# A new order of work and new turns in shared buffers, for four chunks of a transformer stack on one core

## The reference, cut to what matters

```python
x = layernorm(x + L0_attn(x))   # a decaying complex scan along the sequence
x = layernorm(x + L0_ffn(x))    # 8 experts, 256 hidden, top 2 by a sparse mixer
x = layernorm(x + L1_attn(x))   # 2 heads of 64, rotary, causal
x = layernorm(x + L1_ffn(x))    # latent attention (4 heads of 32), then 1 shared + 8 experts, 128 hidden
x = layernorm(x + L2_attn(x))   # 16 heads of 8, window of 32
x = layernorm(x + L2_ffn(x))    # dynamics: router, 2 steps of expert-driven control, refinement
x = layernorm(x + L3_attn(x))   # top 16 of 32 keys looked back at, previous key, phrase key
x = layernorm(x + L3_ffn(x))    # 8 experts, 342 hidden, routed by distance to centroids
```

```python
for _ in range(2):
    ctx = concatenate([integrated, v]); ...
    integrated = integrated + halt * (x_next - integrated)
    v = v + halt * (v_next - v)
refined = gelu(integrated @ refine_w1 + b1) @ refine_w2 + b2
out = xf + integration_weight * refined
```

## Time and profile before

| | us |
|---|---|
| median of 3 runs (lowest, highest) | 1227.08 (1224.92, 1227.92) |
| the profiled execution's own time | 1226.56 |
| its span, first to last instruction | 1224.5 |
| PE busy | 1115.4, 91% of the span |
| PE weight loads busy | 629.4, 51% |
| DVE busy | 827.1, 68% |
| ACT busy | 657.6, 54%, of which 186 table loads are 238.6 |
| POOL busy | 219.1, 18% |
| mean granted clock of PE | 0.959 |

### The profile page before, as it was taken

How to read it: one execution, slowest core, us unless ns; L and a number is a source line. 1 busy time by engine, 2 the same in 40 slices (tenths; PEclk the granted TensorE clock), 3 DMA queues, 4 the chain that set the end, 5 groups by cost and what they waited for, 6 DMA issues and landing times.

```text
span 1224.5 us, 16730 instructions
## 1 busy us (share of the span) xinstructions
PE 1115.4 (91%) x5800; PEld 629.4 (51%) x5800; DVE 827.1 (68%) x2446; ACT 657.6 (54%) x1028; POOL 219.1 (18%) x251
## 2 busy tenths in 40 slices
PE   0799967799999999999799989999999999999996
PEld 0455544566554455554455555454464553565554
DVE  6987566489577369868486696678584774664534
ACT  0225344555756766677666575668546655542321
POOL 1312042224021214131200150005020000202000
PEclk9899989899989989997899999799999999999999
DMA  7021100121110000001001111001001010111210
GB/s 268 4 73 54 39 14 14 30 68 34 33 48 24 27 14 21 20 27 33 1 14 56 37 37 37 1 18 37 18 28 37 18 37 1 45 36 54 79 56 9
DMA packets 45394, 45.91 MB, mean 37 GB/s; under 512 B 2584, under 2 KB 44192, under 8 KB 45056
## 3 DMA queue, kind: packets, MB, share of 16 engines
q1 hardware_dynamic: 42336, 40.59, 10.9%
q10 hardware_dynamic: 2976, 4.26, 1.0%
HBM read 43.79 MB, written 1.05 MB: 37 GB/s over the span
## 4 chain that ended last, share of the span: by engine, by line
PE 77%; DVE 13%; ACT 4%; DMA 3%; issue 2%; POOL 1%; POOLq 0%; DVEq 0%; ACTq 0%
PE bank L450 32%; PE bank L485 13%; PE bank L757 10%; PE bank L780 5%; ACT L1781 2%; PE bank L457 2%; PE bank L525 2%; PE bank L439 2%; PE bank L747 1%; PE bank L792 1%; PE bank L668 1%; DMA xt<-x_in 1%; DVE x L1209 1%; DMA w_exp<-in_ffn 1%; PE bank L508 1%
## 5 line engine op out<-in xcount | busy, mean ns | idle before, releaser
L450 PE MATMUL bank<-xt,w_exp 128*128 128x512 f32 (+1 forms) x784 | 390.6, 629 | 19.1 <-DMA w_exp<-in_ffn 6.4
L1781 ACT ACT_TABLE_LOAD x186 | 238.6, 1283 | 70.9 <-PE bank L450 41.7
L450 PEld LDWEIGHTS bank<-xt,w_exp 128*128 128x128 f32 (+1 forms) x784 | 134.5, 190 | 193.7 <-issue 117.1
L485 PEld LDWEIGHTS bank<-w_exp,hid 128*128 128x128 f32 (+1 forms) x1568 | 189.3, 196 | 52.2 <-issue 15.8
L485 PE MATMUL bank<-w_exp,hid 128*128 128x128 f32 (+1 forms) x1568 | 199.0, 282 | 5.7 <-DVE hid L1192 4.2
L1209 DVE SCALAR_TENSOR_TENSOR x<-bank,dense,x 128x128 f32<-128x128 f32 x384 | 107.9, 343 | 119.4 <-PE bank L485 103.0
L757 PE MATMUL bank<-picked,w_dyn 128*128 128x512 f32 x320 | 142.9, 596 | 0.0
L1818 ACT ACTIVATE hid<-bank,w_cols 114x512 f32<-114x512 f32 x96 | 65.2, 687 | 114.6 <-PE bank L450 114.0
L2187 POOL TENSOR_SCALAR rstd<-mv 128x4 f32<-128x4 f32 x32 | 7.0, 218 | 552.6 <-DVE mv L1075 552.4
L1820 ACT ACTIVATE hid<-bank 128x512 f32<-128x512 f32 x100 | 57.5, 597 | 85.1 <-PE bank L450 84.7
L757 PEld LDWEIGHTS bank<-picked,w_dyn 128*128 128x128 f32 x320 | 59.1, 190 | 74.8 <-issue 74.7
(11 more groups left out here) (288 smaller groups left out, 1515.9 us busy)
## 6 DMA issues: line engine op xcount, KB each, us to landing
w_exp<-in_ffn SPq DMA_DIRECT2D x68, 192.0 KB, 3.2
w_exp<-in_ffn SPq DMA_DIRECT2D x32, 384.0 KB, 3.5
w_exp<-in_ffn SPq DMA_DIRECT2D x32, 342.0 KB, 3.1
w_dyn<-in_dyn ACTq DMA_DIRECT2D x1, 1636.0 KB, 12.1
w_const<-in_const SPq DMA_DIRECT2D x1, 1274.0 KB, 11.7
xt<-x_in SPq DMA_DIRECT2D x4, 256.0 KB, 15.4
out<-x ACTq DMA_DIRECT2D x4, 256.0 KB, 2.3
att<-in_stage SPq DMA_DIRECT2D x1, 512.0 KB, 5.2
```

The source lines that it names most:

```text
L450: nc.tensor.matmul(seqs(bk[0:rows, :]) if len(rhs.shape) == 3 else bk[0:rows, :], lhsT, rhs, start=True, stop=True).then_inc(S[k % STREAMS ...
L485: last = nc.tensor.matmul(bk[:, t * 128:(t + 1) * 128], hid[0:rows, (e * nf + f) % RING_H, t * 128:(t + 1) * 128], ffn_w(k, st, "down", e, ...
L1781: A.preload_act_table_set(name)
```

## The change

`TURNS` of `att` and `ring` are reordered: chunk 2's A comes after chunk 0's C and D1 and chunk 3's A after chunk 0's E; chunk 0's G comes before chunk 3's C and D1; chunk 0's H comes before chunk 3's D2. All four `MERGE` strings and `BANK_OF` are written anew for these turns, with the same number of pieces. In stage F the router's hidden layer, the one-hot rows, and the refinement move out of `dyn` into `nx` and `xt` of the chunk itself; `take("dyn", ...)` moves behind the router (PE and ACT) and disappears from DVE; `dyn` is released when the second step is done (`stepped`) instead of at the residual sum; step 0 begins one tick later. Where two chunks now share one semaphore without the turn between them, a wait for the event before is added (`in_turn`, `oh_ready`).

```diff
 TURNS = {
-    "att": ((0, "A"), (1, "A"), (2, "A"), (3, "A"), (0, "C"), (0, "D1"), (1, "C"), (1, "D1"), (0, "E"), (2, "C"),
-            (2, "D1"), (1, "E"), (3, "C"), (3, "D1"), (0, "G"), (2, "E"), (1, "G"), (3, "E"), (2, "G"), (3, "G")),
-    "ring": ((0, "B"), (1, "B"), (0, "D2"), (2, "B"), (1, "D2"), (3, "B"), (2, "D2"), (3, "D2"), (0, "H"), (1, "H"),
+    "att": ((0, "A"), (1, "A"), (0, "C"), (0, "D1"), (2, "A"), (1, "C"), (1, "D1"), (0, "E"), (3, "A"), (2, "C"),
+            (2, "D1"), (1, "E"), (0, "G"), (3, "C"), (3, "D1"), (2, "E"), (1, "G"), (3, "E"), (2, "G"), (3, "G")),
+    "ring": ((0, "B"), (1, "B"), (0, "D2"), (2, "B"), (1, "D2"), (3, "B"), (2, "D2"), (0, "H"), (3, "D2"), (1, "H"),
             (2, "H"), (3, "H")),
...
 MERGE = dict(
     PE=(
-        "0000000100000011200000000003200000000000000000000231111111101000001100111111101010101010111111111111"
-        "0100000111000010300000111111011000000011101010100000010111110011010101110100001012222222122102000020"
-        "2222202202200202222000002022222022222202200200011111111100001112000000011122221112220000011101111122"
...
+        "0000000000000100000000000101000000000000000000111110100000110011111110100011010111111111111010000011"
+        "1100001110000001010000000000200001111100112200011010101100000012111201122211112222112112212212222220"
+        "0001201220222022002222022222200002020111111021111011000000011100010003000000001100022222002201113222"
...
@@ released
+            if u == "F":
+                return X.stepped, (q, 1)
             return S[q].resid, (q, u)
...
-        oh3 = y(F_CTRL)[:, 0:TILES * 3 * 4 * E8].rearrange("p (t r e) -> p t r e", t=TILES, r=3)
+        def one_hots(s):
+            return flat(s)[:, 0:TILES * 3 * 4 * E8].rearrange("p (t r e) -> p t r e", t=TILES, r=3)
+
+        def refining(s, j):
+            return xtv(s) if j else seqs(flat(s))
...
@@ PE, stage_f
                     if i == 2:
-                        take("dyn", k, "F")
...
                     if i == 4:
                         pe.wait_ge(X.ro_hid.s, X.ro_hid.at(k))
-                        by_token(k, ("F", "logits"), lambda t: y(F_VEL)[0:32, t * 128:(t + 1) * 128],
+                        by_token(k, ("F", "logits"), lambda t: flat(s)[0:32, t * 128:(t + 1) * 128],
                                  part("dyn", "ro_w2")[0:32, :], E8, (T.logits, (k, "F")))
                         yield
+                        take("dyn", k, "F")
...
-                    yield from step(k, 0, i - 3, bks)
+                    yield from step(k, 0, i - 4, bks)
...
@@ DVE, stage_f
                     if i == 7:
-                        take("dyn", k, "F")
...
+                        if X.oh_ready.at(k) > 1:
+                            dve.wait_ge(X.oh_ready.s, X.oh_ready.at(k) - 1)
...
@@ ACT, stage_f
+            def in_turn(sg, *event):
+
+                if sg.at(*event) > 1:
+                    act.wait_ge(sg.s, sg.at(*event) - 1)
...
                     if i == 3:
-                        take("dyn", k, "F")
...
+                        in_turn(X.ro_hid, k)
...
-                    if i == 6:
+                    if i == 4:
                         small_exp(k, "F", TILES * E8)
                         yield
+                        take("dyn", k, "F")
...
                     if i == 53:
                         act.wait_ge(T.filled, T.full(k, "F", "refined"))
-                        A.activation(y(F_REF + 2), T.bank(k, "F", "refined")[:], ACT.Identity, bias=cc(C_RB2),
+                        A.activation(flat(s), T.bank(k, "F", "refined")[:], ACT.Identity, bias=cc(C_RB2),
```

92 lines of the change are left out of this document (46 added, 46 removed).

## The result

The changed kernel takes 1236.24 us (median of 4 runs, 1235.19 to 1237.35), the kernel before 1226.72 in the same comparison: a ratio of 1.0076, 95% interval 1.0063 to 1.0089. Forecast were 1212 us and a range from 1187 to 1247. The time lies inside the range, but on the other side of the kernel before: the sign was wrong.

The account below looks back on a forecast made before the run. PE sets the pace, with 1031 us of unchanged work in 1226.6 us. 1226.6 - 12 (start and C to F) - 7 (G) - 9 + 9 (middle) + 4 (end) = 1211.6, median 0.5 above: 1212 us, range 1187 to 1247.

Parts of the forecast that it names:

- Start, -9: Before chunk 0's C: fewer scans queued on DVE let C begin at 88, loss 38 instead of 47 us.
- From C to F, about -2: Chunks 0 and 1, C to F: cover 185.9, deficits 41.6; chunk 0's `oht` at 319, stretch wins about 2 us.
- D2's turning to chunk 1's first projections: 13.5 of work, no chain: 0: Edge between C and F: 13.5 us of PE work with no chain to wait for, so no loss.
- the old chain times were upper bounds: C to F, chunks 0 and 1: same chain instructions, so old times bound the new; stretch may win up to 20 more.
- G's turn, -7: Chunk 0's G: PE's 6.48 us wait for chunk 3's D1 rows goes; -7, between -4 and -7.
- Half the old stalls go, -9, and +9 for the new short edges: Middle: half of 19 us old stalls go, F's turning to `oht` in chunks 1 and 3 costs 9; bounds -19, +25.
- dyn, 0: Stage F's buffer `dyn` taken later, given sooner: worth 0 in the new order, at most 5 us.
- The middle and the end, +4: Middle's -9 and +9, then the end: tighter edges to chunk 3's G and H cost 4 us.
- H ahead of D2, no change: Chunk 0's H before chunk 3's D2: weights load in another order; no change, at most the old 6.4 us again.
- The clock, 10 us either way: PE's lower clock level falls at other places in the new order: worth 10 us either way, taken in by the range.
- F packed too tightly: Rival: `oht` to `refined` takes 145 us in chunks 0 and 1, over cover 139.5 and 120.5: +30, 1242 us; chance 0.25.
- Nothing comes of it: Rival: start's gain waits later as D1 and C of chunk 1 meet B's products on DVE: +17, 1227 us; chance 0.15.

Follow-up runs that it names:

- the woven one with new turns: Changed kernel with F's short operands filled up to 128 rows by zeros and the whole written order rewoven from traced durations: 1235.63 us, 1.0053 of the kernel before.
- the nine fillers: Changed kernel with nine dense matmuls of weights on weights in TensorE's wait for chunk 2's first dynamics step: 1232.84 us, 1.0040 of the kernel before.

## Why the prediction was wrong, step by step

- *Start, -9.* Right in its size and place: C of chunk 0 at 89.4, forecast 88; the loss is 8 us smaller. TensorE's idle time fell by 5.4 us, which fits the cause given, the queue on VectorE. The rest goes with the clock, 0.95 there before and 1.00 after (3.6 us), which the prediction did not have. D2's turning, forecast by the same sum at 161.8, came at 161.6.
- *From C to F, about -2.* Here the prediction failed, by 19 of the 25 us that it missed: `oht` of chunk 0 at 338.1 instead of 319. Up to D2 every edge holds within 1.1 us. The first step that failed is "D2's turning to chunk 1's first projections: 13.5 of work, no chain: 0". It took 25.6: 5.4 us of waiting for expert weights (2.5 and 2.9), 5.9 lost at the low clock, 1.2 for VectorE. The way of counting failed with it: an edge was its chain or its cover, the cover at full clock. From C's turning to `oht` the granted clock was 0.92 (0.96 before), 20 us instead of 9, and no edge had a term for it. I had priced late weights under the turns as "I take no change, and at most as much again"; they cost this stretch 10.7 us with the new order and 4.0 with the old. Also short: chunk 1's D1 to normalised rows, 42.3 instead of 34.4 (I took chunk 0's time for it, where chunk 1's own in the earlier trace rows, 214.94 to 259.15, was 44.2), and E's projections to F's turning, 59.3 instead of 47.6. My statement that the old chain times were upper bounds is what made these look safe. They are times of a chain with certain work beside it, and the new order put B of chunk 2 beside it; of that, its products on VectorE are 2.3 us by experiment, with one late load just ahead of the turning, 2.95, still in place. F's turning to `oht` was over-priced (14.4 instead of 20.3).
- *G's turn, -7.* Right: the wait of 6.5 us is gone, and TensorE's idle time from 300 to 626 is 8.2 us smaller. "Half the old stalls go, -9, and +9 for the new short edges" is then -1.7 in this stretch, near the 0 that it adds up to.
- *dyn, 0.* Right: 0.9984 alone in the old order. In the new one it is needed and couldn't be priced.
- *The middle and the end, +4.* From `oht` of chunk 0 to the end the loss is 102 us (99 before) where the sum had 96: 6 us, the other part of the miss. The rest behind 853 is -3.2, the clock there +5.6. H of chunk 3 went through without a pause, 81 us before the end (78 forecast), 3 of them for the clock. What the prediction didn't have is the stall of 6.1 us in F of chunk 2: I went through F's edges at `oht` and in the refinement and not through the one between the two steps, which has its own chain over ScalarE and VectorE.
- *H ahead of D2, no change.* The second term that failed; wrong in kind. I looked at SyncE's queue and the slots. What the turn moved was cover: H of chunk 0 left the place of F's late step (work 626 to 701: 80 us before, 96 after, of it 8.4 us idle and up to 10.6 of clock), and H of chunk 1 could not follow, as it stands behind G of chunk 1.
- *The clock, 10 us either way.* Net it is +2.5 to +4 us in the profiled pair, within the bound, and about nothing between typical runs, so it doesn't turn the sign; that the net came out so small is luck. It made most of the gain of the middle (up to -23.6 us, which no step of mine forecast) and cost 31 from 50 to 250 and from 626 on, and it is what makes the late step dear: five idle matmuls there are worth 6.7 us.
- *The rivals.* "F packed too tightly" has the right time (1242) and the wrong place: `oht` to `refined` took 157.5 us in chunk 0 (338.1 to 495.6), longer than its 145, and 136.7 in chunk 1, shorter. Both were over their cover, by 18 and 16 us, but so was chunk 0's before (197 against 173), and the stretch that holds most of both is 25 us faster than before. That the time fell near it is luck. "Nothing comes of it" has the better mechanism, the start's gain that goes on to wait on the way to F, but its cause, VectorE's products, is shown for 2.3 us only.

What stays open: with the late weights away the two kernels are 13.3 us apart, with the late step filled (in the new order alone) 1.7 to 2.8. These don't add up to one account, because each edit moves the clock behind it. I can show what the two places cost locally (6.7 us up to `oht`, 8.4 of idle time and the clock around the late step), not a sum of causes that gives 9.5: the cause of the whole gap stays open. Nor is it settled what the turns would be worth under orders of equal quality.

## What to carry to other kernels

When a change re-orders work, price for each thin stretch what dense work stands beside it before and after, not only the chains' own length: here the loss came where an order had moved the last experts away from a chain (96 us for what took 80), while the waits that the change was made for, at the start and before G, did go. Give the clock a term in each such stretch too. A chain's time measured in one order is no bound for another: late loads and a shared queue come with the new neighbours. And an order rebuilt from durations alone can be 2% slower than the one it is to replace (1261 us where at most 1218 were forecast), with the clock low or with ScalarE's sequence full of table loads; count those, and run it.

## What the runs showed of the hardware

- The granted clock depends on more than whether TensorE has matmuls in flight. The same number of matmuls of the same 512 columns, with the operands' rows filled up from 32 and 64 to 128 by zeros, raises the mean clock from 0.956 to 0.963 and from 0.959 to 0.965, and the kernels are 15 and 12 us faster. The clock accounts for some 9 and 8 us of that; the rest is unexplained.
- In several of these kernels time follows the mean clock at about 1 us for each 0.001: in the run with other banks 1230.5 us at 0.957 and 1244.6 at 0.945, in the woven one with new turns 1230 at 0.974 and 1240 at 0.963. It isn't so in all: in 25 runs of the kernel before, from 0.949 to 0.959, it is about half of that. A comparison of orders to less than 1% has to be read with the clock beside it.
- A float32 matmul of 512 columns is two instructions in these traces: the nine fillers are 18 instructions in 7.99 us, 0.89 us for a matmul, and the two matmuls that the code has for `refined` are four. The 0.43 us of the earlier trace rows are from start to start of such instructions, so a matmul takes 0.86. The bfloat16 picks are one instruction each.
